# A cross-attention kernel on one core: ScalarE's order in the first attention, and the layer norm that follows it

## The reference

```python
def block_0(x, ctx):                       # 16 heads of 32
    h = layer_norm(x)
    q, k, v = h @ q_w + q_b, ctx @ k_w + k_b, ctx @ v_w + v_b
    p = softmax(where(mask, q @ k.T / sqrt(32), smallest))
    x = x + (p @ v) @ cproj_w + cproj_b
    return x + gelu_tanh(layer_norm(x) @ fc_w + fc_b) @ proj_w + proj_b

def block_1(x, ctx):                       # 16 heads of 128, an extra key and value
    for i in (1, 2):
        x = x + attention(layer_norm(x), ctx, weights_i)
    return x + gelu(layer_norm(x) @ w_fc1 + b_fc1) @ w_fc2 + b_fc2
```

## Time and profile before

| | us |
|---|---|
| median of 3 runs | 2335.46 (2335.41 to 2336.28) |
| the profiled execution | 2335.53 |
| its span in the profile | 2333.7 |

### The profile page before, as it was taken

One profiled execution on the slowest core, in us unless ns is written; L12 is line 12 of the kernel. 1 busy time (PEld: TensorE's weight loads), 2 busy tenths in 40 slices (PEclk: granted clock), 3 DMA queues, 4 the chain that ended last, 5 costly groups with the idle time before them and its releaser, 6 DMA issues.

```text
span 2333.7 us, 37085 instructions
## 1 busy us (share of the span) xinstructions
PE 2281.2 (98%) x13091; PEld 2069.4 (89%) x13091; DVE 1335.6 (57%) x3098; ACT 1123.3 (48%) x2468; POOL 366.1 (16%) x731
## 2 busy tenths in 40 slices
PE   6999899999999999999999999999999999999999
PEld 5777778888999999999998898999999999988887
DVE  6777784443656556655654625665565565554743
ACT  4777762354445445444443434445445444452421
POOL 2111126530000100100101120001001001003421
PEclk9999999999999999999999999999999999999999
DMA  5422126575455645645645474545555555544210
GB/s 180 141 74 71 59 82 229 177 241 144 161 185 196 211 153 197 233 143 193 224 148 164 148 218 153 192 159 193 213 182 182 202 191 190 182 149 139 60 55 32
DMA packets 255224, 376.25 MB, mean 161 GB/s; under 512 B 90302, under 2 KB 210514, under 8 KB 255042
## 3 DMA queue, kind: packets, MB, share of 16 engines
q1 hardware_dynamic: 255042, 373.87, 47.4%
HBM read 315.77 MB, written 58.05 MB: 160 GB/s over the span
## 4 chain that ended last, share of the span: by engine, by line
PE 91%; DVE 3%; ACT 3%; issue 2%; DMA 1%; POOL 0%; SPq 0%; ACTq 0%; DVEq 0%
PE ps_k L1630 10%; PE ps_k L1631 10%; PE ps_k L1632 10%; PE ps_o L1630 8%; PE ps_o L1632 8%; PE ps_o L1631 8%; PE ps_v L1630 6%; PE ps_v L1632 6%; PE ps_v L1631 6%; PE ps_s L1630 4%; PE ps_s L1632 4%; PE ps_s L1631 4%; PE ps_t L1814 3%; PE ps_t L1751 1%; PE ps_o L1763 1%
## 5 line engine op out<-in xcount | busy, mean ns | idle before, releaser
L1630 PE MATMUL ps_k<-cs_hi,w_a_hi 128*128 128x376 f32 x1152 | 390.3, 339 | 3.9 <-DVE k_lo L1405 3.7
L1631 PE MATMUL ps_k<-cs_lo,w_a_hi 128*128 128x376 f32 x1152 | 385.2, 334 | 0.0
L1632 PE MATMUL ps_k<-cs_hi,w_a_lo 128*128 128x376 f32 x1152 | 384.2, 334 | 0.0
L1038 ACT ACTIVATE prob<-ps_s,row_columns 112x376 f32<-112x376 f32 x256 | 147.4, 576 | 304.9 <-DVE row_columns L1411 304.8
L815 POOL CAST k_hi<-xk_hi 128x1 fp32r<-128x1 f32 x256 | 47.4, 185 | 1233.0 <-PE ps_s L1632 1233.0
L1630 PEld LDWEIGHTS ps_k<-cs_hi,w_a_hi 128*128 128x128 f32 x1152 | 216.8, 188 | 7.5 <-issue 6.8
L1631 PEld LDWEIGHTS ps_k<-cs_lo,w_a_hi 128*128 128x128 f32 x1152 | 217.1, 188 | 0.5
L1632 PEld LDWEIGHTS ps_k<-cs_hi,w_a_lo 128*128 128x128 f32 x1152 | 216.9, 188 | 0.0
L1405 DVE SCALAR_TENSOR_TENSOR k_lo<-ps_k,col_b,k_hi 128x375 fp32r<-128x375 f32 x256 | 155.2, 606 | 79.1 <-ACT k_hi L1007 73.5
L1007 ACT ACTIVATE k_hi<-ps_k,col_b 128x375 fp32r<-128x375 f32 x256 | 146.4, 572 | 91.2 <-PE ps_k L1632 90.2
L1310 DVE RECIPROCAL row_columns<-row_columns 112x1 f32<-112x1 f32 x384 | 62.4, 163 | 196.4 <-ACT prob L1038 188.5
(11 more groups left out here) (267 smaller groups left out, 5696.5 us busy)
## 6 DMA issues: line engine op xcount, KB each, us to landing
ckd_hi<-context_by_key_halves SPq DMA_DIRECT2D x64, 768.0 KB, 4.4
ckd_lo<-context_by_key_halves SPq DMA_DIRECT2D x64, 768.0 KB, 6.1
cs_hi<-context_halves SPq DMA_DIRECT2D x64, 752.0 KB, 6.1
cs_lo<-context_halves SPq DMA_DIRECT2D x64, 752.0 KB, 7.8
w_raw_b<-in_blocks_b SPq DMA_DIRECT2D x104, 256.0 KB, 4.5
w_raw_a<-in_blocks_a SPq DMA_DIRECT2D x104, 256.0 KB, 4.8
q<-q_scratch SPq DMA_DIRECT2D x72, 224.0 KB, 6.0
extra<-extra_probability SPq DMA_DIRECT2D x16, 896.0 KB, 4.9
```

The source lines that it names most:

```text
L1038: act.activation(prob[buf][0:LQ, 0:KW], ps_s[buf][0:LQ, 0:KW], ACT.Exp, bias=max_neg[0:LQ, buf:buf + 1], accum_out=prob_sum[0:LQ, buf:buf ...
L1630: pe.matmul(out, w_h, m_h, start=first, stop=False)
L1631: pe.matmul(out, w_h, m_l, start=False, stop=False)
L1632: return pe.matmul(out, w_l, m_h, start=False, stop=last)
```

## The change

Four pieces, no instruction added or taken away, the arithmetic unchanged; TensorE's, GpSimd's and SyncE's lists stay as they are.

1. All batches but the last, ScalarE: in tiles 0, 1 and 3 the copy of the third transpose comes before the key's eviction and the copy of the fourth before the third exponential. In tile 2 the second copy comes before the first exponential, the third before the second exponential, and the key's eviction after the fourth copy. VectorE evicts the key's low half one step later: after the second normalization in tiles 0, 1 and 3, and after the fourth maximum in tile 2.
2. The last batch, ScalarE: in tile 0 the fourth transpose is copied right behind the third; the deviations of rows 0 and 1 are taken in tile 3 between the second and the third copy (they came with row 2's after the fourth). VectorE's `key_lo` comes after the fourth maximum.
3. The high and low halves of column 3 of the perceptron's first `w_a` block (`A_M0`) are made at the end of `project` instead of at the end of the last batch.
4. In `project`, ScalarE scales row 4 before the deviation of row 5; VectorE normalizes row 2 before it adds row 4, row 3 next, and the halves and measurements follow in another order.

```diff
+                def tile(place, t):
+                    following = place.key(t + 1)
+                    turned(place, t, 0)
+                    if t == 2:
+                        turned(place, t, 1)
+                        exp(*following, 0)
+                        value_finished(place, t, 0)
+                        turned(place, t, 2)
+                        exp(*following, 1)
+                        turned(place, t, 3)
+                        key_hi(*place.key(t + 2))
+                    else:
+                        exp(*following, 0)
+                        turned(place, t, 1)
+                        exp(*following, 1)
+                        turned(place, t, 2)
+                        key_hi(*place.key(t + 2))
+                        turned(place, t, 3)
+                    exp(*following, 2)
+                    exp(*following, 3)
+                    value_finished(place, t, 3)
+
+                def final_tile(place, t):
+                    following = place.key(t + 1)
+                    for j in range(SUB0):
+                        if not (t == 0 and j == 3):
+                            turned(place, t, j)
+                        if t == 0 and j == 2:
+                            turned(place, t, 3)
+                        if following:
+                            exp(*following, j)
+                        if key_evicted(place, t, j):
+                            key_hi(*key_evicted(place, t, j))
+                        if t == 0:
+                            split_hi(1, place.block_b + 1, (j,), lambda s: (v_mm, 3 * place.batch + 3))
+                        if t == NT - 1 and j == 1:
+                            deviation(1, 0)
+                            deviation(1, 1)
+                    if t == NT - 1:
+                        deviation(1, 2)
...
-                        if place.split_column(t) is not None:
+                        if place.split_column(t) is not None and not (place.final and t == NT - 1):
                             split_hi(0, place.block_a + 1, [place.split_column(t)],
...
                     scaled(norm, 2)
                     scaled(norm, 3)
+                    scaled(norm, 4)
                     deviation(norm, 5)
-                    scaled(norm, 4)
+                    split_hi(0, A_M0, [3], lambda s: (k_mm, NT * NB))
                     deviation(norm, 6)
...
                                 masked_maximum(*following, j)
+                                if j == 3 and place.key(t + 2) and (place.final or t == 2):
+                                    key_lo(*place.key(t + 2))
                                 if j:
                                     normalized_0(*following, j - 1)
-                            if key_evicted(place, t, j):
-                                key_lo(*key_evicted(place, t, j))
+                                if j == 2 and not place.final and t != 2:
+                                    key_lo(*place.key(t + 2))
...
+                    scale(2)
                     add_y(4, 0, 0)
-                    scale(2)
+                    scale(3)
                     halves(norm, 0)
                     measure(norm, 4)
-                    scale(3)
                     halves(norm, 1)
+                    scale(4)
+                    halves(norm, 2)
+                    halves(norm, 3)
                     add_y(5, 0, 0)
-                    halves(norm, 2)
                     measure(norm, 5)
-                    scale(4)
-                    halves(norm, 3)
+                    halves(norm, 4)
+                    scale(5)
                     add_y(6, 0, 0)
                     measure(norm, 6)
-                    scale(5)
-                    halves(norm, 4)
+                    split_lo(0, A_M0, [3])
                     scale(6)
                     halves(norm, 5)
```

24 lines of the change are left out of this document (9 added, 15 removed).

## The result

The changed kernel takes 2321.24 us (median of six runs, 2319.43 to 2322.73) against 2335.43 us (six runs, 2334.54 to 2336.28). The ratio is 0.9939, with an interval of 0.9926 to 0.9952. That is 14.2 us less; 15.8 were forecast. The profiled execution took 2322.3 us with a span of 2320.5, 13.2 less than before.

What follows compares the result with a forecast made beforehand. TensorE, busy 98% of 2333.7 us, was taken as the bound, so only its waits could be won. Terms -11.3 - 3.7 - 0.2 - 0.6 = -15.8 took 2335.5 to 2319.7 us, own range 2316 to 2323.5.

Steps and rivals of the forecast that it cites:

- Batches 1 to 6: Six like batches: copies ahead of key eviction and third exponential gain 1.89 us a batch, -11.3 us; bounds -15 and -6.5.
- (1): Tiles 1 and 3: VectorE's fourth maximum starts at 6.2, so the next wait takes half; 2327 us, chance 0.22.
- (3): Copies still wait for something else, such as the exponentials ahead; 0 to 4 us come, 2333 us, chance 0.06.
- (4): VectorE's key low half and fourth maximum become last in every tile, 0.9 us a tile slower; 2345 us, chance 0.04.
- rival (2): VectorE's normalization gets ahead of GpSimd's instruction and all waits go, TensorE's own pace; 2314.7 us, chance 0.08.
- The normalization beside GpSimd: Tile 2: VectorE's second normalization takes 1.14 us, usually 0.42, while GpSimd splits the context; tile 2 gains only 0.28.
- Batch 0: First batch: tile 0 gains 1.0, tile 1 1.1, tile 2 0.4, tile 3 1.2; -3.7 us, bounds -2 and -5.
- The last batch: Tile 0's fourth copy moved up, next scores held by VectorE's low half of the key; -0.2 us, between -0.9 and +0.7.
- The drop that I half charged: Last batch: a possible clock drop, 1.6 us at most; -0.2 taken between -0.9 and +0.7.
- Deviations and rows 0 to 3: Last weighted sum to third hidden product, 20.36 us before: early square roots let rows start sooner, gain 3.3 us.
- The new wait: Perceptron's first block: late column 3 of `w_a` delays `ctx_raw` in SyncE's queue, so TensorE waits 2.45 us for a Gelu.
- The net of the tail: Behind the last weighted sum: 3.3 gained less 2.45 waited leaves 0.85, taken as -0.6 us; bounds -3.3 and +1.

Runs made afterwards that it cites:

- experiment 7: Changed kernel with VectorE's low half of the key one step earlier again in tiles 0, 1 and 3, ScalarE's new order kept; 2328.80 us, one run.
- experiment 9: Changed kernel without GpSimd's subtractions for the contexts of batches 2 to 7, products left inexact; 2318.73 us, ratio 0.9921 to the kernel before.
- the first profile: The first profiled execution of the changed kernel itself, nothing further altered; 2322.3 us, span 2320.5.
- experiment 3: Kernel before with piece 1 alone, the orders of ScalarE and VectorE in all batches but the last; 2321.87 us, ratio 0.9940.
- experiment 1: The changed kernel run and profiled once more, nothing altered; 2321.15 us over four runs, ratio 0.9938 to the kernel before, span 2319.2.
- experiment 5: Changed kernel with the deviations of rows 0 and 1 after the fourth copy again; 2323.97 us, one run.
- experiment 2: Changed kernel with both halves of column 3 of `w_a` made early, before the last output's halves; 2318.78 us, ratio 0.9928 to the kernel before.
- experiment 11: Kernel with column 3 early and tile 2's low half first, plus an earlier key mask and last-batch splits spread over tiles 0 and 1; 2325.37 us, ratio 0.9953.
- experiments 8: Changed kernel with both engines' lists in tile 2 as before; 2323.57 us, one run.
- experiments 6: Changed kernel with the fourth transpose of the last batch's tile 0 copied after the third exponential again; 2321.66 us, one run.
- 4: Changed kernel with piece 1 undone, so pieces 2 to 4 alone; 2335.33 us over ten runs, ratio 0.9998 to the kernel before.

## Why the prediction was right, and where it was not

- **Batches 1 to 6** (-11.3): -11.6. Batches 1 to 5 gave 1.89 us each, as forecast; all four tiles are within 0.07 us of the walk, VectorE's bound in tile 2 included. Batch 6 gave 2.19: GpSimd subtracts nothing in it, and I had counted it like the others. What was walked for ScalarE was right because VectorE's order moved with it (experiment 7); rivals (1), (3) and (4) fall with tiles 1 and 3 of 7.08 and 6.44 us and a waits view with 0.9 us left in six batches, rival (2) with a tile 2 of 7.31 and not 7.07 us. No run shows the 0.9 us a tile of which (4) is added up; the runs showed tiles within 0.07 us of the walk.
- **The normalization beside GpSimd** was walked in tile 2 with the 1.14 us of the earlier trace rows. It takes 1.21 us in this trace and 0.42 without GpSimd's subtractions (experiment 9), and that is worth 0.30 us a batch (0.23 of it in tile 2). The 0.79 us more is less than one of the four subtractions (4.1 us together). How the one holds the other is not shown by any run.
- **Batch 0** (-3.7): -2.7. Tiles 0 and 1 went as walked (7.49 and 6.39 us). The step that failed is "tile 2 0.4, tile 3 1.2": they gave 0.1 and 0.5. With 6 value products in every tile TensorE has little to do while it waits, and three normalizations of tile 2 meet GpSimd's instructions (80.73, 4.11 us) and take 0.72, 0.50 and 0.94 us (the first and the last below, VectorE's timeline); I had walked it with one. Without the subtractions they take 0.42 us each and half a microsecond comes back (experiment 9). The other half is open: even then the two tiles take 7.00 and 6.82 us, where 6.75 and 6.5 were walked, and no run tells why.

```profile
81.22 0.72 DVE L1350 TENSOR_SCALAR prob<-prob,row_columns 112x375 f32<-112x375 f32 x1
...
84.12 0.94 DVE L1350 TENSOR_SCALAR prob<-prob,row_columns 112x375 f32<-112x375 f32 x1
```

- **The last batch** (-0.2): -0.6, inside its bounds. The walk without a clock drop gave -0.9. The drop that I half charged did not come in the first profile, came in the second where it cost nothing, and came doubled in experiment 3. So the charge was not borne out, and it made the forecast of this stretch worse: without it the walk was 0.3 us too good, with it 0.4 us too poor. No run shows the 1.6 us for a low clock that lie between the -0.9 and the +0.7 of this term, and of which the tail's -0.6 has a part; they were my estimate. What the runs showed is 1.5 us for 3.4 us at a granted clock of 0.50 (experiment 1, at 1215 us), and nothing where TensorE would have waited anyway (experiment 1, at 269.6 us).
- **Deviations and rows 0 to 3** (3.3): 2.9, of which experiment 5 gives 2.5 to the deviations. The first hidden product starts 9.93 us after the last weighted sum, 10.0 were walked; the rest is lost in rows 5 and 6. The square roots start 0.01 us behind the table's load (1.28 us), and TensorE never waited for the copy behind them.
- **The new wait** (2.45): 2.24, by the mechanism that was named, as experiment 2 shows. SyncE's queue was released at 310.4; by the offset of 14.7 us that is 325.1 on the old clock, where 325.0 was said.
- **The net of the tail** (-0.6) is the term that was mis-sized. It came out at +1.05 us in the profiled execution (-14.71 to -13.66) and at -0.7 in experiment 1. The low clock behind the pause costs 1.5 us when it comes; I had it in the bound (+1) and counted a quarter microsecond of it. Of the eight traces that have this pause, four have the low clock behind it, which would be 0.75 us.

The profiled execution is 2.6 us above the forecast: batch 0 (1.0) and the tail (1.65), less the 0.3 and 0.4 us that the like batches and the last batch gave more, and 0.6 us in stretches that no term has (0.2 before the first scores, 0.4 behind the first block). In the trace of experiment 1 the same terms come to -15.6 us, 0.2 from the forecast, but 1.5 us go to a low clock at 1215 us, which no term has, and its first scores start 0.7 us sooner than in the kernel before. So the mechanism was right to a few tenths, batch 0 apart, and how near the time of a run came rests on where the low clock fell.

## What to carry to other kernels

When copies out of a shared bank are moved ahead of other work, walk the second engine's list in the same breath: here VectorE's half of the reordering decides over 6.5 of 14 us. A step that is moved takes its semaphore with it, and so every transfer queued behind the wait on it: 0.6 us of VectorE's work set down 14 us later cost a pause of 2.0 to 2.2 us of the 3.5 us that the last batch and the projection had gained, and where a low clock followed it all of them. Work that is moved off one late chain has another deadline, which stands in TensorE's list and not in the waits of before (experiment 11).

## What the runs showed that was not expected

The same pieces have TensorE's low clock (a granted clock of 0.50 to 0.52 of full) in different places. Behind the pause for the Gelu (at 319 to 336 us) it came after 1.92, 2.24, 2.48 and 2.50 us (experiment 5, the first profile, experiments 8 and 7) and stayed away after 1.35, 2.02, 2.14 and 2.59 us (experiments 6, 1, 4 and 9). So the pause's length doesn't decide it. The stretches behind the shortest with it and the longest without it, experiments 5 and 9:

```profile
325.00:328.40 3.40, 3.40 (x12) 3.40 (x12) 2.37 (x3) 2.02 (x5) 3.40 (x3) 0.50 0.38 106
321.50:324.90 3.40, 3.40 (x20) 3.40 (x21) 2.38 (x4) 3.33 (x7) 2.96 (x2) 1.00 0.55 164
```

In five of the fourteen traces it came at 1214 to 1230 us, where the longest wait was 1.1 us and the kernel before keeps its full clock. It lasts 3.4 us, once in each of experiments 3 and 11 6.8, and 3.4 us of it cost 1.5 unless TensorE would have waited anyway. What decides where it falls is not shown by any run.

The first scores start between 58.2 and 59.8 us from run to run, long before any changed instruction. The changed kernel's ten runs lie within 3.3 us. A difference of 2 us between two single executions or two single spans of this kernel therefore shows nothing; the lengths of its tiles, which repeat within a few hundredths of a microsecond, do.
